# A threshold search by six false-position counts in place of a 31-bit bisection

## The chip, the cores and the metric

One Trainium2 chip, one core. The metric is device time in microseconds (us) of one execution, lower is better.

## What is computed

The kernel takes 2048 tokens of width 1024 through two branches that are added to the input. The part that the change touches is the first branch: for each token it keeps the 1376 of 2752 gate values that are largest in magnitude and sets the others to zero.

```python
s = jax.nn.silu(jnp.einsum('bsh,ih->bsi', x, w_gate))      # 4 x 512 tokens, 2752 units
k = int(K_FACTOR * I)                                      # 1376
_, idx = jax.lax.top_k(-jnp.abs(s), k)
flat = flat.at[rows, idx.reshape(B * S, k)].set(0.0)
s = s * jnp.einsum('bsh,ih->bsi', x, w_up)
return jnp.einsum('bsi,hi->bsh', s, w_down)
...
x = x + _L0_attn_ref(xn, ...) + _L0_ffn_ref(xn, ...)       # second branch: MLP + routed latent + layernorm
```

## The kernel before

**Blocks and granules.** The tokens are worked in four blocks `b` of 512, each as four tiles of 128 tokens. A block is a list of granules `m` (the class `Plan`). A plain granule is one 128-row slice of weights: TensorE makes 4 tiles x 3 matmuls of 512 columns with it, the three being the high-by-high, high-by-low and low-by-high parts of a float32 product (`product`, L1065 to L1067). In blocks 1 to 3 the gate steps and three of the six up steps go in four "fast" pairs: 28 granules each, seven products (`q`, 0 to 6) of four granules, each granule 2 x 3 matmuls. Granules of products 1, 3, 5 and 6 take "mixed" weights: they are loaded as one float32 tile, ScalarE writes its high part (L1026), GpSimd then subtracts to get the low part (L850; in pairs 0 to 2, VectorE makes it for product 6, L1542), and only then can TensorE use the granule. In block 0 every weight is split into its two parts on the chip: while the search runs, GpSimd alone does it, with a `tensor_scalar` (L841) and a `tensor_tensor` (L845) per granule.

**Order.** There is no scheduler. Each engine walks over the same granules and, at the granules that `Plan` names, emits its other work in a fixed order; it then runs in order and waits on semaphores alone. An engine can run ahead of TensorE in this list, or fall behind. ScalarE also evacuates banks: latent (L973), hidden as relu (L982) and square (L994), routed (L986). There are two sets of four PSUM banks, and most steps alternate between them, so a step's banks must be read before the next but one opens.

**The search.** Once all magnitudes `mag` of a block are there (2816 per token, 64 of them padding of -1), the threshold `thr` is found bit by bit from bit 30 down: 31 steps. In each, VectorE counts two token tiles (`search_bit`, L1414) and ScalarE the other two (`count`, L901, a Sign with an accumulated sum); both read `cand`. Then `settle` refuses or keeps the bit with two instructions on 128x4 elements (L1403, L1406). After the last, `drop_ties` counts four tiles once more (L1422) and enters a branch only if more than 1376 are left. `mask` (L1481) applies the threshold, and GpSimd multiplies gate by up (L874) before TensorE turns the product for the last matmuls.

**Where the steps stand.** In block 0 the search begins at granule 52 and its steps are three granules apart. In blocks 1 to 3 it begins ten granules after pair 2 ends, that is at granule 9 of the 28 of the last fast pair (counted from 0); the next steps are 7 and 14 granules later, then every 11/4 granules. The third step would stand in the middle of the last mixed granules, and one line moves ScalarE's part of it to the end of the fast part:

```python
            self.count_at[last] = self.count_at.pop(steps_at[2])
```

## Time and profile before

| | |
|---|---|
| runs | 2320.54 us median of 3 (2317.87 to 2321.05) |
| profiled execution, span from first to last instruction | 2316.5 us |
| its own time with what lies around the span | not given with the profile; the median is 4.0 us above the span |
| TensorE busy | 2300.8 us (99%) |
| VectorE, ScalarE, GpSimd busy | 1674.1, 1112.2, 927.2 us |
| granted TensorE clock | full in all 40 slices |

Engines in the rows are PE (TensorE), DVE (VectorE), ACT (ScalarE), POOL (GpSimd). Matmuls are pipelined: one has a duration of 0.39 us, but the next starts about 0.23 us after it, so durations overlap and the starts are what to read. A row names a source line, the operation, the tiles written and read, shape and number of instructions.

### The profile page before, as it was taken

How to read it: one execution, taken by the hardware profiler on the slowest of the kernel's cores; microseconds unless marked ns; L12 is line 12 of the kernel's file. 1: busy time of each engine (PE TensorE's matmuls, PEld its weight loads, DVE VectorE, ACT ScalarE, POOL GpSimd, SP SyncE). 2: the span in 40 equal slices, each digit the busy share in tenths (PEclk: the TensorE clock that was granted, in tenths of full speed). 3: DMA queues.
4: the chain of work that ended last, by engine and by line, in shares of the span. 5: the costliest groups of instructions: out<-in, count | busy, mean ns of one | idle time of the engine just before them, and what ended most of it. 6: DMA issues, size and time to landing. Idle time of an engine off the chain costs nothing.

```text
span 2316.5 us, 27959 instructions
## 1 busy us (share of the span) xinstructions
PE 2300.8 (99%) x10432; PEld 1912.1 (83%) x10432; DVE 1674.1 (72%) x1834; ACT 1112.2 (48%) x1307; POOL 927.2 (40%) x746
## 2 busy tenths in 40 slices
PE   8999999999999999999999999999999999999999
PEld 6888888888888888888888888888888888888887
DVE  4349999986366999998334599998723569999850
ACT  3247776223243688822124379780213457976110
POOL 5468988797354321333024423035004441302600
PEclk9999999999999999999999999999999999999999
DMA  7798988868899765575678875556567886555655
GB/s 285 276 402 315 334 320 305 266 238 310 300 361 331 244 227 191 195 248 178 235 232 277 283 253 193 197 193 242 203 221 254 282 268 239 192 192 195 232 191 179
DMA packets 202184, 583.61 MB, mean 252 GB/s; under 512 B 21568, under 2 KB 30784, under 8 KB 200512
## 3 DMA queue, kind: packets, MB, share of 16 engines
q1 hardware_dynamic: 202048, 581.82, 72.8%
q8 instruction: 83, 1.36, 0.2%
q14 instruction: 53, 0.43, 0.1%
HBM read 446.40 MB, written 135.33 MB: 251 GB/s over the span
## 4 chain that ended last, share of the span: by engine, by line
PE 82%; DVE 10%; DMA 3%; issue 2%; ACT 1%; SPq 1%; POOL 1%; DVEq 0%; ACTq 0%
PE bank L1065 26%; PE bank L1067 26%; PE bank L1066 26%; DVE junk_v L1414 3%; DVE prod L1481 2%; PE bank L1085 2%; DVE junk_v L1422 2%; DMA mixed_w<-mixes 1%; DMA split_w<-w 1%; DVE prod L1344 1%; PE bank L1076 1%; DVE acc L1385 0%; DMA w<-mixed_w 0%; SPq L631 0%; SPq L627 0%
## 5 line engine op out<-in xcount | busy, mean ns | idle before, releaser
L1414 DVE TENSOR_SCALAR_CACHE_REDUCE junk_v<-mag,cand 128x2816 bf16<-128x2816 f32 x248 | 780.3, 3146 | 8.8
L901 ACT ACTIVATE junk_s<-mag,cand 128x2816 uint8<-128x2816 f32 x248 | 655.9, 2645 | 191.6 <-DVE cand L1406 172.9
L1065 PE MATMUL bank<-w,tok 128*128 128x512 f32 (+1 forms) x808 | 309.9, 384 | 0.2 <-POOL w L845 0.2
L1067 PE MATMUL bank<-w,tok 128*128 128x512 f32 (+1 forms) x808 | 308.3, 381 | 0.0
L1066 PE MATMUL bank<-w,tok 128*128 128x512 f32 (+1 forms) x808 | 308.0, 381 | 0.0
L845 POOL TENSOR_TENSOR w<-raw,w 128x512 fp32r<-128x512 f32 (+1 forms) x196 | 267.9, 1370 | 76.5 <-ACT w L889 66.7
L1065 PE MATMUL bank<-w,prod_t 128*128 128x512 f32 x672 | 269.4, 401 | 0.0
L1067 PE MATMUL bank<-w,prod_t 128*128 128x512 f32 x672 | 262.8, 391 | 0.0
L1066 PE MATMUL bank<-w,prod_t 128*128 128x512 f32 x672 | 261.9, 390 | 0.0
L859 POOL TENSOR_TENSOR squares<-squares 128x512 f32<-128x512 f32 x64 | 67.4, 1054 | 463.9 <-ACT hidden L994 463.9
L1065 PE MATMUL bank<-tok,w 128*128 128x512 f32 x640 | 249.0, 389 | 0.0
L1066 PE MATMUL bank<-tok,w 128*128 128x512 f32 x640 | 249.0, 389 | 0.0
L1067 PE MATMUL bank<-tok,w 128*128 128x512 f32 x640 | 249.0, 389 | 0.0
L1054 ACT ACTIVATE prod_t<-bank 128x512 fp32r<-128x512 f32 x88 | 52.4, 596 | 346.4 <-PE bank L1085 346.4
L850 POOL TENSOR_TENSOR w<-w 128x512 fp32r<-128x512 f32 x96 | 149.1, 1576 | 137.6 <-ACT w L1026 137.3
L1065 PE MATMUL bank<-w,hidden 128*128 128x512 f32 x512 | 199.2, 389 | 0.0
L1066 PE MATMUL bank<-w,hidden 128*128 128x512 f32 x512 | 199.2, 389 | 0.0
L1067 PE MATMUL bank<-w,hidden 128*128 128x512 f32 x512 | 199.2, 389 | 0.0
L874 POOL TENSOR_TENSOR prod<-prod,mag 128x512 f32<-128x512 f32 x88 | 130.9, 1509 | 145.2 <-DVE prod L1481 144.9
L1065 PEld LDWEIGHTS bank<-w,tok 128*128 128x128 f32 x808 | 151.7, 188 | 27.0 <-POOL w L845 0.5
L1067 PEld LDWEIGHTS bank<-w,tok 128*128 128x128 f32 x808 | 151.6, 188 | 26.9
L1066 PEld LDWEIGHTS bank<-w,tok 128*128 128x128 f32 x808 | 151.7, 188 | 26.1
(166 smaller groups left out, 4066.5 us busy)
## 6 DMA issues: line engine op xcount, KB each, us to landing
w<-split_w SPq DMA_DIRECT2D x498, 512.0 KB, 3.4
split_w<-w SPq DMA_DIRECT2D x188, 512.0 KB, 5.3
w_more<-split_w SPq DMA_DIRECT2D x66, 512.0 KB, 5.3
w<-mixed_w SPq DMA_DIRECT2D x126, 256.0 KB, 3.6
w_more<-mixed_w SPq DMA_DIRECT2D x66, 256.0 KB, 3.5
rows<-x_dram SPq DMA_DIRECT2D x32, 512.0 KB, 5.4
raw<-w_down_dram SPq DMA_DIRECT2D x44, 256.0 KB, 4.1
raw<-w_up_dram SPq DMA_DIRECT2D x40, 256.0 KB, 3.2
```

The source lines that it names most:

```text
L845: pool.tensor_tensor(lo, words, hi, ALU.subtract).then_inc(lo_ready, 1)
L850: pool.tensor_tensor(slot_of(g)[:, 1, :], slot_of(g)[:, 1, :].bitcast(F32), slot_of(g)[:, 0, :], ALU.subtract).then_inc(pool_lo, 1)
L859: pool.tensor_tensor(squares[:, n, :], squares[:, n, :], squares[:, n, :], ALU.mult).then_inc(squared, 1)
L874: pool.tensor_tensor(prod[:, c, :, units], prod[:, c, :, units], mag[:, c, :, units], ALU.mult).then_inc(prod_ready, 1)
L901: act.activation(junk_s[:, :, :], mag[:, :, t, :], ACT.Sign, scale=-1.0, bias=cand[:, t:t + 1], accum_out=cnt[:, t:t + 1]).then_inc(counte ...
L1054: act.activation(prod_t[0][:, c, :], banks[bank][:, :], ACT.Copy).then_inc(operand_hi, 1)
L1065: pe.matmul(out, left[0], right[0], start=first, stop=False)
L1066: pe.matmul(out, left[0], right[1], start=False, stop=False)
L1067: return pe.matmul(out, left[1], right[0], start=False, stop=last)
L1085: last = pe.transpose(banks[bank][:, t * P:(t + 1) * P], prod[:, c, t, :], ident[:, :])
L1414: dve.tensor_scalar(junk_v[:, :, :], mag[:, :, t, :], cand[:, t:t + 1], float(1 - (GATED - KEPT)), ALU.is_lt, ALU.add, accum_out=cnt[:, t: ...
L1422: dve.tensor_scalar(junk_v[:, :, :], mag[:, :, t, :], thr[:, t:t + 1], None, ALU.is_ge, ALU.add, accum_out=cnt[:, t:t + 1]).then_inc(searc ...
```

## The change

The search starts from the mean magnitude of each token: VectorE sums one tile (1 instruction), ScalarE three. Then six counts follow at points found by false position (a secant between an upper and a lower point), each with a `settle` of nine instructions on 128x4 to 128x16 elements. A token whose count comes within 3 of the aim keeps its point. Then for each of the four tiles VectorE zeroes what is not below the point (2816 elements) and takes the eight largest of the rest; the threshold is one of these, chosen by how far the count was off. The 31-step bisection stands only in the branch, entered when two values tie at the threshold or when a token's count is still more than 3 off. ScalarE now counts three token tiles and VectorE one, in every step. The steps are four granules apart in block 0; in blocks 1 to 3 they stand at granules 9 (mean), 16 and 23 of the last fast pair and then every three granules. The line that moved ScalarE's part of the third step is gone.

```diff
+COUNTS = 6
+NEAR = 3
+AIM = KEPT - 1 - NEAR
+ROUND = 1.5 * 2 ** 23
...
-            steps_at += [last + 3 + (11 * k + 3) // 4 for k in range(BITS + 1 - len(steps_at))]
+            steps_at += [last + 3 + 3 * k for k in range(COUNTS + 2 - len(steps_at))]
         else:
             first = last + 5 if later else end[("gate", GC - 2)] + LAG + 1
-            steps_at = [first + 3 * k + (0 if later else k // 8) for k in range(BITS + 1)]
-        self.search_at = {m: k for k, m in enumerate(steps_at[:BITS])}
-        self.search_from, self.search_end = first, steps_at[BITS]
-
-        self.count_at = {m: k for m, k in self.search_at.items()}
-        if later and FAST[b] > SPILLED_PAIR:
-            self.count_at[last] = self.count_at.pop(steps_at[2])
+            steps_at = [first + 4 * k for k in range(COUNTS + 2)]
+        self.mean_at = self.search_from = first
+        self.search_at = {m: k for k, m in enumerate(steps_at[1:COUNTS + 1])}
+        self.search_end = steps_at[COUNTS + 1] + 3 * TILES + 1
+        self.pick_at = {steps_at[COUNTS + 1] + 3 * t: t for t in range(TILES)}
+        self.pick_from = steps_at[COUNTS + 1]
+        self.count_at = {first: -1, **self.search_at}
...
-NV = TILES // 2
+NV = 1
 NS = TILES - NV
 VECTOR_TILES, SCALAR_TILES = range(NV), range(NV, TILES)
+WIDTH = GK * P
+OFF = WIDTH // 2 - AIM
+assert NEAR == 3
...
-                if k or n:
-                    act.wait_ge(counted, (b * BITS + k) * NS + n)
-                act.activation(junk_s[:, :, :], mag[:, :, t, :], ACT.Sign, scale=-1.0,
-                               bias=cand[:, t:t + 1], accum_out=cnt[:, t:t + 1]).then_inc(counted, 1)
+                if b or k >= 0 or n:
+                    act.wait_ge(counted, (b * (COUNTS + 1) + k + 1) * NS + n)
+                if k < 0:
+                    act.activation(junk_s[:, :, :], mag[:, :, t, :], ACT.Copy,
+                                   accum_out=cnt[:, t:t + 1]).then_inc(counted, 1)
+                else:
+                    act.activation(junk_s[:, :, :], mag[:, :, t, :], ACT.Sign, scale=-1.0,
+                                   bias=tried[:, 0, t:t + 1], accum_out=cnt[:, t:t + 1]).then_inc(counted, 1)
...
+            def start_search(b):
+
+                at = b * SEARCHES
+                dve.wait_ge(mag_ready, (b + 1) * MAG_STEPS)
+                dve.memset(ends[:, 0, 0, :], 0.0).then_inc(search, 1)
+                dve.memset(ends[:, 0, 1, :], float(GATED - AIM)).then_inc(search, 1)
+                dve.memset(ends[:, 1, 1, :], -float(AIM)).then_inc(search, 1)
+                for i, t in enumerate(VECTOR_TILES):
+                    dve.wait_ge(search, at + 3 + i)
+                    dve.tensor_scalar(junk_v[:, :, :], mag[:, :, t, :], 1.0, None, ALU.mult, ALU.add,
+                                      accum_out=cnt[:, t:t + 1]).then_inc(search, 1)
+
+            def first_guess(b):
+
+                at = b * SEARCHES + 3 + NV
+                dve.wait_ge(counted, (b * (COUNTS + 1) + 1) * NS)
+                dve.wait_ge(search, at)
+                dve.tensor_scalar(ends[:, 1, 0, :], cnt[:, :], float(PAD), 2.0 / GATED, ALU.add,
+                                  ALU.mult).then_inc(search, 1)
+                dve.tensor_scalar(tried[:, 0, :], cnt[:, :], float(PAD), 0.75 / GATED, ALU.add,
+                                  ALU.mult).then_inc(search, 1)
+
+            def away(b, k):
+
+                dve.wait_ge(counted, (b * (COUNTS + 1) + k + 2) * NS)
+                dve.wait_ge(search, b * SEARCHES + searched(k) + NV)
+                dve.scalar_tensor_tensor(out=tried[:, 1, :], in0=cnt[:, :], scalar=-float(2 * OFF), in1=weight[:, :],
+                                         op0=ALU.add, op1=ALU.mult).then_inc(search, 1)
+
             def settle(b, k):
 
                 at = b * SEARCHES + searched(k) + NV
-                bit = 1 << (BITS - 1 - k)
-                after = cand if k + 1 < BITS else thr
-                dve.wait_ge(counted, (b * BITS + k + 1) * NS)
-                dve.wait_ge(search, at)
-                dve.tensor_scalar(refused[:, :], cnt[:, :], float(PAD + 1), float(bit), ALU.is_gt,
-                                  ALU.mult).then_inc(search, 1)
+                away(b, k)
                 dve.wait_ge(search, at + 1)
-                dve.scalar_tensor_tensor(out=after[:, :].bitcast(I32), in0=cand[:, :].bitcast(I32), scalar=bit >> 1,
-                                         in1=refused[:, :], op0=ALU.bitwise_or, op1=ALU.bitwise_xor).then_inc(search, 1)
-
-            def search_bit(b, k):
+                dve.tensor_scalar(outside[:, 0, :], tried[:, 1, :], NEAR + 0.25, None, ALU.is_gt).then_inc(search, 1)
+                dve.tensor_scalar(outside[:, 1, :], tried[:, 1, :], -NEAR - 0.25, None, ALU.is_lt).then_inc(search, 1)
+                dve.wait_ge(search, at + 3)
+                dve.copy_predicated(ends[:, :, :, :], outside[:, :, None, :].to_broadcast([P, 2, 2, TILES]),
+                                    tried[:, None, :, :].to_broadcast([P, 2, 2, TILES])).then_inc(search, 1)
+                dve.wait_ge(search, at + 4)
+                dve.tensor_tensor(apart[:, :, :], ends[:, 1, :, :], ends[:, 0, :, :], ALU.subtract).then_inc(search, 1)
+                dve.wait_ge(search, at + 5)
+                dve.reciprocal(share[:, :], apart[:, 1, :]).then_inc(search, 1)
+                dve.wait_ge(search, at + 6)
+                dve.tensor_tensor(share[:, :], share[:, :], ends[:, 0, 1, :], ALU.mult).then_inc(search, 1)
+                dve.wait_ge(search, at + 7)
+                dve.tensor_tensor(share[:, :], share[:, :], apart[:, 0, :], ALU.mult).then_inc(search, 1)
+                dve.wait_ge(search, at + 8)
+                dve.tensor_tensor(tried[:, 0, :], ends[:, 0, 0, :], share[:, :], ALU.subtract).then_inc(search, 1)
+
+            def search_step(b, k):
 
                 at = b * SEARCHES + searched(k)
                 for i, t in enumerate(VECTOR_TILES):
                     dve.wait_ge(search, at + i)
-                    dve.tensor_scalar(junk_v[:, :, :], mag[:, :, t, :], cand[:, t:t + 1], float(1 - (GATED - KEPT)),
-                                      ALU.is_lt, ALU.add, accum_out=cnt[:, t:t + 1]).then_inc(search, 1)
+                    dve.tensor_scalar(junk_v[:, :, :], mag[:, :, t, :], tried[:, 0, t:t + 1],
+                                      float(2 * OFF - (WIDTH - AIM)), ALU.is_lt, ALU.add,
+                                      accum_out=cnt[:, t:t + 1]).then_inc(search, 1)
+
+            def last_away(b):
+
+                at = b * SEARCHES + PICKED
+                away(b, COUNTS - 1)
+                dve.wait_ge(search, at - 2)
+                dve.tensor_scalar(share[:, :], tried[:, 1, :], 0.25, ROUND, ALU.add, ALU.add).then_inc(search, 1)
+                dve.wait_ge(search, at - 1)
+                dve.tensor_scalar(share[:, :], share[:, :], ROUND, -1.0, ALU.subtract, ALU.mult).then_inc(search, 1)
...
+            def largest_below(b, t):
+
+                at = b * SEARCHES + PICKED + 2 * t
+                dve.wait_ge(search, at)
+                dve.scalar_tensor_tensor(out=below[:, :, :], in0=mag[:, :, t, :], scalar=tried[:, 0, t:t + 1],
+                                         in1=mag[:, :, t, :], op0=ALU.is_lt, op1=ALU.mult).then_inc(search, 1)
+                dve.wait_ge(search, at + 1)
+                dve.max(largest[:, t, :], below[:, :, :].rearrange("p k n -> p (k n)")).then_inc(search, 1)
...
             def drop_ties(b):
...
+                choose(b)
...
                 with dve.If(excess > 0):
...
+                    with dve.Fori(0, BITS):
...
-                    if m == plan.search_from:
-                        dve.wait_ge(mag_ready, (b + 1) * MAG_STEPS)
-                        dve.memset(cand[:, :].bitcast(I32), 1 << (BITS - 1)).then_inc(search, 1)
+                    if m == plan.mean_at:
+                        start_search(b)
                     if m in plan.search_at:
                         if plan.search_at[m]:
                             settle(b, plan.search_at[m] - 1)
-                        search_bit(b, plan.search_at[m])
+                        else:
+                            first_guess(b)
+                        search_step(b, plan.search_at[m])
+                    if m == plan.pick_from:
+                        last_away(b)
+                    if m in plan.pick_at:
+                        largest_below(b, plan.pick_at[m])
                     if m == plan.search_end:
-                        settle(b, BITS - 1)
                         drop_ties(b)
```

ScalarE, block 1, from the last evacuation before the search to the first plain step, before (`junk_s,cnt` are counts, `w`/`w_more` are high parts of mixed granules, `latent` is the first plain step's evacuation):

```order
L940 ACTIVATE prod<-bank 128x4x128 x2
L901 ACTIVATE junk_s,cnt<-mag,cand 128x2816 x2
L1026 ACTIVATE w_more<-w_more 128x512 x4
L901 ACTIVATE junk_s,cnt<-mag,cand 128x2816 x2
L1026 ACTIVATE w<-w 128x512 x2
L1026 ACTIVATE w_more<-w_more 128x512 x4
L1026 ACTIVATE w<-w 128x512 x2
L901 ACTIVATE junk_s,cnt<-mag,cand 128x2816 x8
L973 ACTIVATE latent_58<-bank 128x512 x4
```

and the same place now:

```order
L969 ACTIVATE prod<-bank 128x4x128 x2
L927 ACTIVATE junk_s,cnt<-mag 128x2816 x3
L1055 ACTIVATE w_more<-w_more 128x512 x4
L930 ACTIVATE junk_s,cnt<-mag,tried 128x2816 x3
L1055 ACTIVATE w<-w 128x512 x2
L1055 ACTIVATE w_more<-w_more 128x512 x2
L930 ACTIVATE junk_s,cnt<-mag,tried 128x2816
L1055 ACTIVATE w_more<-w_more 128x512
L930 ACTIVATE junk_s,cnt<-mag,tried 128x2816
L1055 ACTIVATE w_more<-w_more 128x512
L930 ACTIVATE junk_s,cnt<-mag,tried 128x2816
L1055 ACTIVATE w<-w 128x512 x2
```

Three counts stand where two stood, ahead of the first four high parts and ahead of the last eight; and three more counts now lie between the fourth and the seventh of those eight, where none lay.

VectorE, block 0, one settle and the count after it, before (`cand` is the point tried):

```order
L1379 TENSOR_TENSOR latent_59<-bank,latent_58 128x512 x4
L1403 TENSOR_SCALAR refused<-cnt 128x4
L1406 SCALAR_TENSOR_TENSOR cand<-cand,refused 128x4
L1414 TENSOR_SCALAR junk_v,cnt<-mag,cand 128x2816 x2
```

and now (`tried` is the point tried):

```order
L1408 TENSOR_TENSOR latent_59<-bank,latent_58 128x512 x4
L1451 SCALAR_TENSOR_TENSOR tried<-cnt,weight 128x4
L1459 TENSOR_SCALAR outside<-tried 128x4
L1460 TENSOR_SCALAR outside<-tried 128x4
L1462 COPY_PREDICATED ends<-outside,tried 128x16
L1465 TENSOR_TENSOR apart<-ends 128x8
L1467 RECIPROCAL share<-apart 128x4
L1469 TENSOR_TENSOR share<-share,ends 128x4
L1471 TENSOR_TENSOR share<-share,apart 128x4
L1473 TENSOR_TENSOR tried<-ends,share 128x4
L1480 TENSOR_SCALAR junk_v,cnt<-mag,tried 128x2816
```

Two dependent small instructions between a count and the next became nine, and one large one went.

ScalarE, block 0, from the evacuation of hidden step 1 to that of routed step 0, before:

```order
L982 ACTIVATE squares<-bank 128x512 x4
L994 ACTIVATE hidden_55<-squares 128x512
L901 ACTIVATE junk_s,cnt<-mag,cand 128x2816
L994 ACTIVATE hidden_55<-squares 128x512
L901 ACTIVATE junk_s,cnt<-mag,cand 128x2816
L986 ACTIVATE acc<-bank,route 128x512 x4
```

and now:

```order
L1011 ACTIVATE squares<-bank 128x512 x4
L1023 ACTIVATE hidden_55<-squares 128x512
L930 ACTIVATE junk_s,cnt<-mag,tried 128x2816 x2
L1023 ACTIVATE hidden_55<-squares 128x512
L930 ACTIVATE junk_s,cnt<-mag,tried 128x2816
L1015 ACTIVATE acc<-bank,route 128x512 x4
```

The whole sixth count, three instructions, stands ahead of the evacuation of routed step 0.

## Rows read from the trace of the kernel before

**Rows 1.** The page: span, busy time by engine, granted clock in tenths.

```profile
span 2316.5 us, 27959 instructions
...
PE 2300.8 (99%) x10432; PEld 1912.1 (83%) x10432; DVE 1674.1 (72%) x1834; ACT 1112.2 (48%) x1307; POOL 927.2 (40%) x746
...
PEclk9999999999999999999999999999999999999999
```

**Rows 2.** PE's waits: us in total, times, longest.

```profile
PE bank L1076 <- DVE rows L1235: 8.7, 2, 7.8
PE bank L1065 <- POOL w L850: 1.6, 4, 0.6
```

**Rows 3.** Groups on DVE, whole span: busy us, mean ns of one.

```profile
L1414 DVE TENSOR_SCALAR_CACHE_REDUCE junk_v<-mag,cand 128x2816 bf16<-128x2816 f32 x248 | 780.3, 3146 | 8.8
...
L1422 DVE TENSOR_SCALAR_CACHE_REDUCE junk_v<-mag,thr 128x2816 bf16<-128x2816 f32 x16 | 50.3, 3147 | 0.6
...
L1344 DVE SCALAR_TENSOR_TENSOR prod<-positive,prod 128x2048 f32<-128x2048 uint8 x9 | 23.8, 2643 | 0.0
```

**Rows 4.** ACT in order of time, block 1: start us, us.

```profile
765.20 2.65 ACT L901 ACTIVATE junk_s<-mag,cand 128x2816 uint8<-128x2816 f32 x1 [2.08 <-DVE cand L1564]
768.03 2.65 ACT L901 ACTIVATE junk_s<-mag,cand 128x2816 uint8<-128x2816 f32 x1
770.68 2.18 ACT L1026 ACTIVATE w_more<-w_more 128x512 fp32r<-128x512 f32 x4
...
780.70 1.14 ACT L1026 ACTIVATE w<-w 128x512 fp32r<-128x512 f32 x2
```

**Rows 5.** POOL in order of time, block 1, the first low parts.

```profile
771.37 5.05 POOL L850 TENSOR_TENSOR w_more<-w_more 128x512 fp32r<-128x512 f32 x4 [8.38 <-ACT w_more L1026]
```

**Rows 6.** PE in order of time, block 1: fast granule 12, first plain granule.

```profile
773.12 0.39 PE L1065 MATMUL bank<-w_more,sums 128*128 128x512 f32 x1
...
794.88 0.39 PE L1065 MATMUL bank<-tok,w 128*128 128x512 f32 x1
```

**Rows 7.** DVE in order of time, block 1: first settle.

```profile
772.67 1.28 DVE L1403 TENSOR_SCALAR refused<-cnt 128x4 int32<-128x4 f32 x1
773.99 1.21 DVE L1406 SCALAR_TENSOR_TENSOR cand<-cand,refused 128x4 int32<-128x4 int32 x1
```

**Rows 8.** Blocks 2 and 3: first count on ACT, fast granule 12 on PE.

```profile
1329.35 2.65 ACT L901 ACTIVATE junk_s<-mag,cand 128x2816 uint8<-128x2816 f32 x1 [2.17 <-DVE cand L1564]
...
1337.27 0.39 PE L1065 MATMUL bank<-w_more,sums 128*128 128x512 f32 x1
...
1893.06 2.64 ACT L901 ACTIVATE junk_s<-mag,cand 128x2816 uint8<-128x2816 f32 x1 [2.17 <-DVE cand L1564]
...
1900.98 0.39 PE L1065 MATMUL bank<-w_more,sums 128*128 128x512 f32 x1
```

**Rows 9.** Settles on DVE, groups in 167 to 260 us (block 0).

```profile
L1403 DVE TENSOR_SCALAR refused<-cnt 128x4 int32<-128x4 f32 x10 | 6.8, 685 | 0.5
L1406 DVE SCALAR_TENSOR_TENSOR cand<-cand,refused 128x4 int32<-128x4 int32 x10 | 5.2, 521 | 0.3
```

**Rows 10.** The same in 796 to 850 us (block 1, POOL mostly idle).

```profile
L1403 DVE TENSOR_SCALAR refused<-cnt 128x4 int32<-128x4 f32 x8 | 1.3, 167 | 0.6
L1406 DVE SCALAR_TENSOR_TENSOR cand<-cand,refused 128x4 int32<-128x4 int32 x8 | 1.3, 164 | 0.3
```

**Rows 11.** Groups on ACT in 167 to 260 us (block 0).

```profile
L901 ACT ACTIVATE junk_s<-mag,cand 128x2816 uint8<-128x2816 f32 x22 | 58.2, 2643 | 23.7 <-DVE cand L1406 19.8 <-DVE cand L1564 3.2
L994 ACT ACTIVATE hidden<-squares 128x512 fp32r<-128x512 f32 x8 | 5.0, 625 | 0.0
...
L982 ACT ACTIVATE squares<-bank 128x512 f32<-128x512 f32 x8 | 4.2, 592 | 0.0
...
L973 ACT ACTIVATE latent<-bank 128x512 fp32r<-128x512 f32 x4 | 2.0, 592 | 0.0
```

**Rows 12.** Block 0: first count on ACT; PE opens shared step 0 (granule 80).

```profile
167.84 2.64 ACT L901 ACTIVATE junk_s<-mag,cand 128x2816 uint8<-128x2816 f32 x1 [3.23 <-DVE cand L1564]
...
250.85 0.39 PE L1065 MATMUL bank<-w,hidden 128*128 128x512 f32 x1
```

More of the change, by code:

```diff
@@ L400 @@
 MAG_STEPS = (GC - 1) + 4
+SETTLES = 9
 def searched(k):
[L405 to L408 removed]
+    return 3 if k < 0 else 3 + NV + 2 + k * (NV + SETTLES)
+PICKED = searched(COUNTS - 1) + NV + 3
+SEARCHES = PICKED + 2 * TILES + 9
 def program(nc, x, w_gate, w_up, w_down, up_w, down_w, fc1_w, expert_w, fc2_w, gamma, beta, routed_w, y):
@@ L485, in program @@
         ident = sb("ident", [P, P], F32)
-        junk_v = sb("junk_v", [P, GK, P], BF16)
-        junk_s = sb("junk_s", [P, GK, P], U8)
+        below = sb("below", [P, GK, P], F32)
+        junk_at = nc.sbuf_base - GK * P * 4
+        junk_v = over("junk_v", [P, GK, P], BF16, junk_at)
+        junk_s = over("junk_s", [P, GK, P], U8, junk_at + GK * P * 2)
+        after_at = junk_at + GK * P * 3
+        chosen = over("chosen", [P, TILES, 8], F32, after_at)
+        picked = over("picked", [P, TILES, 8], F32, after_at + 128)
+        runner = over("runner", [P, TILES], F32, after_at + 256)
+        cand = over("cand", [P, TILES], F32, after_at + 288)
+        refused = over("refused", [P, TILES], I32, after_at + 320)
+        taken = over("taken", [P, TILES], I32, after_at + 352)
+        neg = over("neg", [P, TILES], F32, after_at + 384)
+        bit_f = over("bit_f", [P, 1], F32, after_at + 416)
+        bit_i = over("bit_i", [P, 1], I32, after_at + 448)
+        ends = sb("ends", [P, 2, 2, TILES], F32)
+        tried = sb("tried", [P, 2, TILES], F32)
+        outside = sb("outside", [P, 2, TILES], I32)
+        apart = sb("apart", [P, 2, TILES], F32)
+        share = sb("share", [P, TILES], F32)
+        weight = sb("weight", [P, TILES], F32)
+        place = sb("place", [P, 8], F32)
+        largest = sb("largest", [P, TILES, 8], F32)
         thr = sb("thr", [P, TILES], F32)
-        cand = sb("cand", [P, TILES], F32)
         cnt = sb("cnt", [P, TILES], F32)
-        refused = sb("refused", [P, TILES], I32)
-        taken = sb("taken", [P, TILES], I32)
         extra = sb("extra", [P, TILES], F32)
@@ new lines, in choose @@
+            def choose(b):
+                at = b * SEARCHES + PICKED + 2 * TILES
+                dve.wait_ge(search, at)
+                dve.tensor_tensor(chosen[:, :, :], place[:, None, :].to_broadcast([P, TILES, 8]),
+                                  share[:, :, None].to_broadcast([P, TILES, 8]), ALU.is_equal).then_inc(search, 1)
+                dve.wait_ge(search, at + 1)
+                dve.tensor_tensor(picked[:, :, :], chosen[:, :, :], largest[:, :, :], ALU.mult).then_inc(search, 1)
+                dve.wait_ge(search, at + 2)
+                dve.tensor_reduce(thr[:, :], picked[:, :, :], AX.X, ALU.add).then_inc(search, 1)
+                dve.wait_ge(search, at + 3)
+                dve.tensor_tensor(picked[:, :, 0:7], chosen[:, :, 0:7], largest[:, :, 1:8], ALU.mult).then_inc(search, 1)
+                dve.wait_ge(search, at + 4)
+                dve.tensor_reduce(runner[:, :], picked[:, :, 0:7], AX.X, ALU.add).then_inc(search, 1)
+                dve.wait_ge(search, at + 5)
+                dve.tensor_tensor(extra[:, :], thr[:, :], runner[:, :], ALU.is_equal).then_inc(search, 1)
+                dve.wait_ge(search, at + 6)
+                dve.tensor_reduce(most[:, 0:1], extra[:, :], AX.X, ALU.max).then_inc(search, 1)
+                dve.wait_ge(search, at + 7)
+                dve.transpose(most_t[:, :], most[:, :]).then_inc(search, 1)
+                dve.wait_ge(search, at + 8)
+                dve.tensor_reduce(ties[:, :], most_t[:, :], AX.X, ALU.max).then_inc(search, 1)
@@ L1519, in _ @@
             dve.memset(most[:, :], 0.0).then_inc(constants_set, 1)
-            dve.wait_ge(constants_set, 1)
+            dve.memset(weight[:, 0:NV], -1.0).then_inc(constants_set, 1)
+            dve.memset(weight[:, NV:TILES], -0.5).then_inc(constants_set, 1)
+            for i in range(8):
+                dve.memset(place[:, i:i + 1], float(i - NEAR if i < 7 else 100)).then_inc(constants_set, 1)
+            dve.wait_ge(constants_set, 11)
             normalise(0, 0, 1)
```

41 lines of the change are left out of this document (24 added, 17 removed).

## The prediction

> **What bounds the kernel now.** I read the page first: TensorE is busy for 2300.8 of 2316.5 us at full clock, so the search is hidden unless an engine that feeds TensorE comes late [rows 1]. Busy time alone hides gaps in overlapped matmuls, so I looked at its waits next: 8.7 us at the start of the program, and 1.6 us for low parts of mixed weights made by GpSimd (L850) [rows 2]. Then at its starts: from fast granule 12 to the first plain granule of block 1 it takes 794.88 - 773.12 = 21.76 us for 16 granules, 1.36 us each, without a hole, hence 2.72 us for a plain granule [rows 6]. The reader is to see that nothing is to be won from less search work except those few microseconds, and that every delay of what TensorE waits for is paid in full, since it never catches up.
>
> How near is such a delay? In block 1 ScalarE starts its two counts at 765.20 us, and only after both, at 770.68, makes the high parts of granules 12 to 15 [rows 4]. GpSimd makes the first low part from 771.37; four take 5.05 us, 1.26 each, so it is done at 772.63 [rows 5]. TensorE opens granule 12 at 773.12 [rows 6]. **0.5 us is all the slack.** Blocks 2 and 3 have the same distance from first count to granule 12: 7.92 us, as block 1 has [rows 4, 6, 8].
>
> **Removed.** VectorE had 248 counts of 3.15 us and 16 last counts [rows 3]; 28 large passes and 32 picking instructions replace them. ScalarE's 248 counts become 84. As TensorE hides all of it, the gain is nothing, at most the 1.6 us of [rows 2]. I take 0.
>
> **Term 1, blocks 1 to 3, three counts in front of mixed granules.** A count costs ScalarE 768.03 - 765.20 = 2.83 us [rows 4]. From the order of the changed kernel:
>
> - Mean: three instead of two, and two more memsets (0.2 us, estimated): 765.4 + 8.5 = 773.9. First high part (a quarter of 2.18 us, plus its fill, 0.6) done at 774.5, first low part at 775.8: granule 12 starts about 2.8 us late. GpSimd's 1.26 us per granule then keeps up with 1.36.
> - Count at granule 16: ScalarE 776.0 to 784.5, high parts of 20 to 23 until 786.7. Granule 20 was due at 773.12 + 8 x 1.36 = 784.0, is now due at 786.8, and its low part comes at 786.5: no more loss. Before, those parts began at 780.70 [rows 4].
> - Settle, from 784.6: nine dependent instructions. Undisturbed they cost 0.165 us and a gap of about 0.04 each, 1.85 us in all [rows 10]. But GpSimd makes four low parts back to back from 785.2 to 790.3. In that same situation the two small instructions of the first settle took 1.28 and 1.21 us, not 0.17, and ended at 773.95 and 775.20, just behind the ends of GpSimd's instructions (771.37 + 1.26 n) [rows 5, 7]. Three of the nine get through before GpSimd starts; of the other six, all but the reciprocal wait for one GpSimd instruction each. `tried` is ready at about 790.4.
> - Count at granule 23, in the middle of the last eight mixed granules, where the removed line had kept it away: ScalarE needs 790.4 to 793.2 for the first tile, then the part of granule 24, low part at 795.1, against a due time of 792.2: 2.9 us more. The second and third tile stand before 25 and 26 and cost 2.83 + 0.6 = 3.4 us of ScalarE per granule of 1.36, 2 us more each. The last two parts follow at once. TensorE leaves the fast part at about 804.6 in place of 794.88: **9.8 us**.
>
> With an undisturbed settle (`tried` at 786.5) the same sum gives 1.2 + 2.0 in place of 2.9 + 2 + 2, in all 6.0 us. These are the ends, 6.0 and 9.8; I take 9.8, because the disturbed rows are from the same place. Three blocks: **29.4 us** (18 to 30).
>
> **Term 2, block 0.** GpSimd splits all weights here and is seldom idle, and the settles show it: 0.685 us for the first of the two small instructions and 0.52 for the second, against 0.167 and 0.164 [rows 9, 10]. Nine of them, eight disturbed: 0.69 + 7 x 0.52 + 0.16 + 9 x 0.035 = 4.8 us. ScalarE's list: mean from 168.0 [rows 12], 8.5 us; guess 1.3; count 8.5; latent evacuation 2.0 and VectorE's part behind it 0.6 [rows 11]; settle 4.8; count 8.5; settle 4.8; count 8.5 (to 215.6); relu of hidden 2.0; count with a square [rows 11] from settle's end at 220.4, 9.1; settle 4.8; count with a square 9.1 (to 243.4); relu of hidden step 1, 2.0; settle beside it; sixth count 248.2 to 257.3 with its square. Only then comes the evacuation of routed step 0 (0.7 for its first bank): 258.0. TensorE opens shared step 0 into that bank at 250.85 [rows 12]. **7.2 us.** (Relu of hidden step 1 frees its first bank at 244.0, for granule 76 due at 250.85 - 4 x 2.72 = 240.0: 4 of the 7 us are lost there already.) Lower end: settles of 1.85 us take 15.7 us off, no wait. Upper end: each of eight small instructions waits for a whole GpSimd instruction (about 1 us, midway between 0.6 and 1.3), settle 8.5 us, five settles, 18 us more: 25.
>
> The SBUF page of the Trainium skill (Who interferes with whom) says that a VectorE instruction with two SBUF inputs, or in a 2-port mode, and a GpSimd instruction that reads SBUF exclude each other for their whole length, while counts with an accumulator do not. By that rule the settles behave as in my upper end when GpSimd never pauses, and [rows 5, 7] agree; [rows 9] show about half of it, since GpSimd pauses in block 0.
>
> **Picks.** Two passes per tile. The nearest row for the first is 2.275 to 2.64 us for 2048 elements [rows 3], so 3.1 to 3.6 for 2816; the eight-largest pass has no row of that size: from 3.1 (one element at a time, as a count) to twice that. 25 to 40 us per block, then nine small instructions. In blocks 1 to 3 they end by about 905 us at the latest (851 for the last count, 40, and settles); the first bank behind them is shared step 0's, wanted again at 804.6 + 48 x 2.72 = 935: hidden. In block 0 they hold up GpSimd for 12 us, whose lead on TensorE I take as a few granules: 0 to 5 us, taken as 0, since the waits of term 2 let GpSimd get ahead first.
>
> **What is behind the waiting VectorE in blocks 1 to 3.** After the fast part a step is 8.5 + 1.85 us against 8.16 for three granules. Behind it stands the latent evacuation, at about 840.5; its banks are wanted at 804.6 + 16 x 2.72 = 848.1. Hidden by 7 us; with settles over 3.5 us this would wait too.
>
> **Sum.** 2316.5 + 29.4 + 7.2 = 2353.1 us of span, and 4.0 us above the span as the median of before stands: **2357, I say 2356 us**. This kernel's runs tell 0.2% (4.6 us) from no change.
>
> **Rivals.**
> 1. *Settles undisturbed in the fast part*, the block 0 wait small: 3 x 6.0 + 0 to 4, giving 2338 to 2343. For it: GpSimd takes only 1.26 us at a time. Against it: [rows 7]. 0.2.
> 2. *Block 0 much worse*: settles at their upper end, picks delaying GpSimd: 2320.5 + 29.4 + 18 to 28 = 2368 to 2378. 0.14.
> 3. *Search hidden, no change or faster* (other side): ScalarE's late start is taken up if the first high parts need not wait, that is if the distance from first count to granule 12 exceeded 8.7 + 0.6 + 1.3 = 10.6 us; it is 7.92 [rows 4, 6]. The search would then be free and the 1.6 us of [rows 2] gone: 2319. Only if the mean pass cost under 1.9 us per tile. 0.04 for no change, 0.01 for faster.
> 4. *The change doesn't do what it says*: six counts do not bring every token within 3, and a block takes the branch, 31 x (4 x 3.15 + 2) = 450 us, some 100 of it hidden: 2700 or more. Worked in float32 on the reference's inputs, 11 of 2048 tokens are more than 3 off after the fifth count, none after the sixth, and no threshold ties. On 16 other draws 3 of 64 blocks would fail. It falls in only if ScalarE's sum of magnitudes is off. 0.05.
>
> Forecast, 2346 to 2366: 0.56. The range of 8 in 10 reaches to rivals 1 and 2: 2335 to 2372. Slower 0.94, same 0.05, faster 0.01, from the same cases.
>
> **What would show it.** In each of blocks 1 to 3 TensorE waits for low parts (L850's place) at fast granules 12, 24, 25 and 26, 2.8, 2.9, 2 and 2 us; one ScalarE count between the parts of 23 and 24; small instructions of 1.2 us in the settle before it. In block 0 a wait of TensorE for the relu and then for routed's evacuation, at 240 to 258 us. ScalarE and VectorE busy time down to some 670 and 1040 us with no gain. Wrong if TensorE shows no wait at granule 12 (term 1), if settles in block 0 take 2 us (term 2), or if VectorE runs thousands of instructions in the branch.

## The result, and the profile after

The changed kernel takes **2357.54 us** (median of 4 runs, 2356.5 to 2363.61) against 2319.2 us for the kernel before on the same chips (4 runs, 2317.78 to 2321.05): ratio **1.0172, 95% interval 1.0157 to 1.0186**, slower. Forecast were 2356 us, 2335 to 2372.

The page of its profiled execution (2358.46 us), lines as in [rows 1]:

```profile
span 2356.7 us, 26924 instructions
...
PE 2314.2 (98%) x10432; PEld 1917.6 (81%) x10432; DVE 1039.0 (44%) x1384; ACT 671.0 (28%) x979; POOL 945.0 (40%) x746
...
PEclk9999999999999999999999999999999999999999
```

VectorE lost 635 us of work and ScalarE 441, and the program is 40.2 us longer. In tenths the granted clock still looks full everywhere. TensorE's longest waits, as in [rows 2] (us in total, times, longest):

```profile
PE bank L1094 <- POOL w_more L875: 14.1, 9, 2.2
PE bank L1105 <- DVE rows L1264: 8.6, 2, 7.7
PE bank L1094 <- POOL w L870: 6.7, 4, 4.0
PE bank L1094 <- POOL w L875: 4.9, 7, 1.5
PE bank L1094 <- ACT acc L1015: 3.6, 1, 3.6
```

The 8.6 us at the start were there before. L875 is the low part of mixed weights (before L850), L870 that of block 0's weights (L845), L1015 the evacuation of routed (L986). New are 14.1 + 4.9 - 1.6 = 17.4 us in the fast parts and 3.6 + 6.7 = 10.3 us in block 0: 27.7 of 40.2. The page of waits does not show the rest.

To find it I set the start of each matmul against that of the same matmul before. This lag grows in two kinds of places only: **15.0 us in block 0** (from 250 to 296 us) and **9.2, 8.4 and 8.3 us in the fast parts** of blocks 1 to 3, 25.9 together; elsewhere it stays within 1 us. TensorE in order of time at the end of block 1's fast part (start us, us):

```profile
809.62 0.50 PE L1094 MATMUL bank<-w_more,tok 128*128 128x512 f32 x1 [2.19 <-POOL w_more L875]
...
812.76 0.80 PE L1094 MATMUL bank<-w_more,tok 128*128 128x512 f32 x1 [1.36 <-POOL w_more L875]
813.36 0.63 PE L1095 MATMUL bank<-w_more,tok 128*128 128x512 f32 x1
813.78 0.63 PE L1096 MATMUL bank<-w_more,tok 128*128 128x512 f32 x1
...
819.64 0.39 PE L1094 MATMUL bank<-tok,w 128*128 128x512 f32 x1
```

The reader is to see two things. TensorE waits for low parts; and behind the last wait matmuls start 0.42 us apart (813.36 to 813.78) instead of 0.23: the lower clock level, 1.2 GHz for 2.4. The windows of the same trace show it (from:to, length, busy us of PE, PEld, DVE, ACT, POOL, granted clock, DMA share, GB/s):

```profile
800.00:811.00 11.00, 8.81 (x39) 6.87 (x37) 10.83 (x12) 7.38 (x9) 6.18 (x5) 1.00 0.73 222
811.00:819.70 8.70, 7.11 (x21) 4.90 (x20) 1.25 (x3) 4.03 (x5) 3.77 (x3) 0.61 0.04 8
```

At 0.61 of the clock, 8.7 us lose some 3.4 us. Waits and slow matmuls together make the lag: in the fast parts 25.9 - 17.4 = 8.5 us are slow matmuls, in block 0 15.0 - 10.3 = 4.7. Not all of that is the clock's price: where the next low part is late anyway, a slow matmul only fills time that would have been a wait.

ScalarE and GpSimd in the same place, as in [rows 4, 5]:

```profile
780.78 2.55 ACT L927 ACTIVATE junk_s<-mag 128x2816 uint8<-128x2816 f32 x1 [2.13 <-DVE ends L1431]
...
788.80 2.17 ACT L1055 ACTIVATE w_more<-w_more 128x512 fp32r<-128x512 f32 x4
790.88 2.63 ACT L930 ACTIVATE junk_s<-mag,tried 128x2816 uint8<-128x2816 f32 x1
...
804.96 2.64 ACT L930 ACTIVATE junk_s<-mag,tried 128x2816 uint8<-128x2816 f32 x1 [3.62 <-DVE tried L1473]
...
807.61 0.61 ACT L1055 ACTIVATE w_more<-w_more 128x512 fp32r<-128x512 f32 x1
808.13 2.63 ACT L930 ACTIVATE junk_s<-mag,tried 128x2816 uint8<-128x2816 f32 x1
...
810.75 0.61 ACT L1055 ACTIVATE w_more<-w_more 128x512 fp32r<-128x512 f32 x1
```

```profile
789.49 5.03 POOL L875 TENSOR_TENSOR w_more<-w_more 128x512 fp32r<-128x512 f32 x4 [10.97 <-ACT w_more L1055]
799.86 2.56 POOL L875 TENSOR_TENSOR w<-w 128x512 fp32r<-128x512 f32 x2 [5.33 <-ACT w L1055]
802.36 2.55 POOL L875 TENSOR_TENSOR w_more<-w_more 128x512 fp32r<-128x512 f32 x2
808.30 1.27 POOL L875 TENSOR_TENSOR w_more<-w_more 128x512 fp32r<-128x512 f32 x1 [3.39 <-ACT w_more L1055]
```

Low parts follow high parts by a fill and 1.27 us; a high part of 0.61 us stands behind each count of 2.8. And the settle between the counts, on VectorE, disturbed and, one step later, not:

```profile
799.98 1.21 DVE L1465 TENSOR_TENSOR apart<-ends 128x8 f32<-128x8 f32 x1
801.22 0.18 DVE L1467 RECIPROCAL share<-apart 128x4 f32<-128x4 f32 x1
801.44 1.00 DVE L1469 TENSOR_TENSOR share<-share,ends 128x4 f32<-128x4 f32 x1
802.47 1.21 DVE L1471 TENSOR_TENSOR share<-share,apart 128x4 f32<-128x4 f32 x1
803.72 1.21 DVE L1473 TENSOR_TENSOR tried<-ends,share 128x4 f32<-128x4 f32 x1
...
821.12 0.17 DVE L1465 TENSOR_TENSOR apart<-ends 128x8 f32<-128x8 f32 x1
```

Block 0 holds what I had not sized. GpSimd (three pieces) and then VectorE in order of time. `raw_more` are tiles on which GpSimd makes four subtractions in a row that serve no granule of this stretch:

```profile
251.30 1.04 POOL L884 TENSOR_TENSOR squares<-squares 128x512 f32<-128x512 f32 x1 [4.25 <-ACT hidden L1023]
...
265.73 3.45 POOL L866 TENSOR_SCALAR w<-raw 128x512 fp32r<-128x512 f32 x1
...
273.62 3.98 POOL L870 TENSOR_TENSOR w<-raw,w 128x512 fp32r<-128x512 f32 x1
277.57 0.61 POOL L866 TENSOR_SCALAR w<-raw 128x512 fp32r<-128x512 f32 x1
278.26 1.29 POOL L870 TENSOR_TENSOR w<-raw,w 128x512 fp32r<-128x512 f32 x1
...
284.18 1.28 POOL L849 TENSOR_TENSOR raw_more<-raw_more 128x512 f32<-128x512 f32 x1
...
288.03 1.26 POOL L854 TENSOR_TENSOR raw_more<-raw_more 128x512 f32<-128x512 f32 x1
```

```profile
264.78 3.92 DVE L1497 SCALAR_TENSOR_TENSOR below<-mag,tried 128x2816 f32<-128x2816 f32 x1
268.74 3.10 DVE L1500 MAX8 largest<-below 128x8 f32<-128x2816 f32 x1
...
272.97 3.50 DVE L1497 SCALAR_TENSOR_TENSOR below<-mag,tried 128x2816 f32<-128x2816 f32 x1
```

Under each first pass of a pick (two SBUF inputs) one GpSimd instruction takes 3.3 to 4.0 us instead of 0.6 to 1.3, and ends 0.5 to 1.1 us behind the pass; below I call this a lock. The four locks take 10.5 us of GpSimd above the usual lengths (2.3, 2.8, 2.7 and 2.7). GpSimd had also stood still behind relus that ScalarE owed it: three waits for `hidden`, 8.5 us, of which 3.8 end at 216 us, 4.2 at 251 us and 0.5 at 257 us. And behind the locks come the four subtractions on `raw_more`, 5.1 us. TensorE's longest wait in the picks stands right behind them:

```profile
291.27 0.50 PE L1094 MATMUL bank<-w,hidden 128*128 128x512 f32 x1 [3.99 <-POOL w L870]
```

### The profile page after: what moved, and what is told of

Same layout as the page of the kernel before. It is cut to its first block, busy times and chain, and to the rows that moved or that the text cites. A ratio compares the mean times of both kernels' runs of the same rounds, so it can differ in the third digit from the quotient of the medians.

```text
span 2356.7 us, 26924 instructions
## 1 busy us (share of the span) xinstructions
PE 2314.2 (98%) x10432; PEld 1917.6 (81%) x10432; DVE 1039.0 (44%) x1384; ACT 671.0 (28%) x979; POOL 945.0 (40%) x746
## 3 DMA queue, kind: packets, MB, share of 16 engines
q8 instruction: 83, 1.36, 0.2%
## 4 chain that ended last, share of the span: by engine, by line
PE 87%; ACT 4%; POOL 3%; DVE 3%; issue 2%; DMA 1%; DVEq 0%; POOLq 0%; SPq 0%; ACTq 0%
PE bank L1094 28%; PE bank L1096 28%; PE bank L1095 28%; ACT junk_s L930 2%; PE bank L1114 2%; POOL w L870 1%; ACT junk_s L927 1%; POOL w L866 1%; PE bank L1105 1%; DVE positive L1356 0%; POOL squares L884 0%; DVE prod L1373 0%; DMA w<-mixed_w 0%; POOL w L875 0%; DMA mixes<-w_up_dram 0%
## 5 line engine op out<-in xcount | busy, mean ns | idle before, releaser
L870 POOL TENSOR_TENSOR w<-raw,w 128x512 fp32r<-128x512 f32 (+1 forms) x196 | 274.3, 1403 | 79.6 <-ACT w L914 69.8
L884 POOL TENSOR_TENSOR squares<-squares 128x512 f32<-128x512 f32 x64 | 84.3, 1317 | 430.7 <-ACT hidden L1023 430.7
L1414 DVE TENSOR_TENSOR acc<-bank,acc 128x512 f32<-128x512 f32 x64 | 43.4, 691 | 404.4 <-PE bank L1096 404.4
L1094 PE MATMUL bank<-w,hidden 128*128 128x512 f32 x512 | 201.0, 393 | 10.3 <-POOL w L870 6.7
L930 ACT ACTIVATE junk_s<-mag,tried 128x2816 uint8<-128x2816 f32 x72 | 190.2, 2641 | 71.4 <-DVE tried L1473 67.1
L875 POOL TENSOR_TENSOR w<-w 128x512 fp32r<-128x512 f32 x96 | 146.3, 1547 | 150.0 <-ACT w L1055 149.7
```

Of the source, the lines that this page charges most:

```text
L870: pool.tensor_tensor(lo, words, hi, ALU.subtract).then_inc(lo_ready, 1)
L875: pool.tensor_tensor(slot_of(g)[:, 1, :], slot_of(g)[:, 1, :].bitcast(F32), slot_of(g)[:, 0, :], ALU.subtract).then_inc(pool_lo, 1)
L884: pool.tensor_tensor(squares[:, n, :], squares[:, n, :], squares[:, n, :], ALU.mult).then_inc(squared, 1)
L930: act.activation(junk_s[:, :, :], mag[:, :, t, :], ACT.Sign, scale=-1.0, bias=tried[:, 0, t:t + 1], accum_out=cnt[:, t:t + 1]).then_inc(co ...
L1094: pe.matmul(out, left[0], right[0], start=first, stop=False)
L1414: dve.tensor_tensor(acc[:, t, cols], banks[bank][:, :], acc[:, t, cols], ALU.add).then_inc(bank_emptied[bank], 1)
```

## Experiments

"Block 0" and "fast parts" are the lag of TensorE over the kernel before gained there, in us, in the profiled run. "Ratio" is that to the kernel before on the same chip; e1 to e4 have one run each, against one of 2320.09 us. The slow matmuls behind one and the same wait differ by some 1.6 us from run to run, and some runs lose 5 us at their start (e2, e8), so the places of a single run are compared, and not its time alone.

| run | time, us | ratio, 95% interval | block 0 | fast parts |
|---|---|---|---|---|
| the change | 2357.54 | 1.0172 (1.0157 to 1.0186) | 15.0 | 25.9 |
| e1 search behind the fast part | 2333.01 | one run | 14.8 | 0.0 |
| e2 removed line restored | 2348.57 | one run | 15.6 | 10.2 |
| e3 two tiles on each engine | 2341.62 | one run | 13.5 | 10.2 |
| e4 first pass with one SBUF input | 2353.00 | one run | 7.4 | 26.9 |
| e5 picks 8 granules apart | 2356.6 | 1.0165 (1.0148 to 1.0182) | 12.2 | 25.8 |
| e6 block 0's steps 6 apart | 2343.52 | 1.0107 (1.009 to 1.0124) | 0.0 | 25.8 |
| e7 e1 + e6 + e5 | 2317.8 | 0.9994 (0.9985 to 1.0004) | 0.0 | 0.0 |
| e8 third step behind the fast part | 2343.77 | 1.0103 (1.0086 to 1.012) | 16.4 | 8.6 |
| e9 picks 14 granules later | 2349.02 | 1.0134 (1.0117 to 1.0151) | 7.2 | 25.5 |
| e10 block 0's steps 5 apart | 2349.95 | 1.0134 (1.0117 to 1.0151) | 6.9 | 25.6 |

**e1.** Is all of the 26 us in where the first steps stand?

```diff
-            steps_at = [first, first + 7, first + 14]
-            steps_at += [last + 3 + 3 * k for k in range(COUNTS + 2 - len(steps_at))]
+            first = last + 3
+            steps_at = [first + 4 * k for k in range(COUNTS + 2)]
```

> Blocks 1 to 3 search only after the fast part: first step three granules behind its end, then every four granules; block 0 as in the changed kernel. Theory (ScalarE's counts stand in front of and between the high parts of mixed granules): the fast parts lose nothing, 25.9 us less than the changed kernel, about 2332 us; block 0 still loses 15. Rival (three counts a step are too much for ScalarE anywhere, the loss only moves to the plain steps): above 2345 us, with waits of TensorE for evacuations by ScalarE.

2333.01 us, and the lag does not change by 0.01 us in any of the three fast parts. Term 1 is a matter of place, not of work; nothing behind the fast part pays for the later search. Block 0 still loses 14.8.

**e2.** The removed line alone, restored as quoted above from the kernel before.

> The changed kernel with the removed line back: ScalarE's part of the step at granule 23 stands at the end of the fast part. Theory: the wait at granule 12 (2.2 us) stays, those at 24 to 27 and the slow matmuls behind them go, 6.2 to 7 us in each of three blocks: 2338 to 2340 us. Rival (the disturbed settle of VectorE is what costs, wherever the counts stand): the loss stays near 9 us a block, above 2350.

2348.57 us, above the expectation. 4.8 us of it were lost in the first 40 us of the program, which the edit cannot reach: 2.1 in longer waits of the first transposes for `rows` (10.7 us in 4, in the change 8.6 in 2), and the granted clock was 0.79 from 28 to 36 us, where the change has 1.00. In the fast parts the lag is 3.9, 3.9 and 2.3 us: the waits at granules 24 to 26 are gone, granule 12 is late by 2.2 us as before, the rest is slow matmuls. So the line is worth 4.4 to 6.0 us per block; without the 4.8 us at the start the run would stand at 2343.8, still 4 us over the expectation, which had forgotten the slow matmuls behind granule 12 (1.7 us in two blocks).

**e8.** The whole third step behind the fast part, settle and VectorE's count too: `steps_at = [first, first + 7]` and the rest after `last`.

> Blocks 1 to 3: the third step (mean, first count, second count) stands behind the fast part on both engines; no settle and no count is left among the last mixed granules. Theory (the loss is in counts in front of high parts): granule 12 still costs 2.2 us and the slow matmuls behind it, the 5 to 6 us behind it go, 3 x 2.5 to 4 us remain with block 0's 15: 2343 to 2348. It also tells whether the 5 us lost at the start of the program in the run with the restored line come again (then 2348 to 2353).

2343.77 us (2340.77 to 2347.04), fast parts 2.4, 3.9 and 2.4. It tells the same as e2, so the settle by itself costs nothing where no ScalarE count is queued in front of high parts. The profiled run, the slowest of its four, again lost some 5 us in its first 40 us. Two of its runs are near 2341 us and two at 2346 and 2347, so e2's odd 4.8 are most likely a variation of the start and not the edit's.

**e3.** `NV = 2`, two token tiles on each of ScalarE and VectorE.

> The changed kernel with two token tiles counted by each engine, positions unchanged. Theory: no wait at granule 12 (two counts fit in its 7.9 us), but the step at granule 23 still stands between the parts: 3.8 + 2 us a block, 5 to 6 in place of 8.6, and no wait for routed's evacuation in block 0 (3.8 less); picks as before: 2343 to 2349 us. Rival (only the place of the counts matters, not how many): above 2353.

2341.62 us. No wait at granule 12 (two sums fit in the 7.92 us of [rows 4, 6, 8]), 3.4 us in each block from 24 to 26, no wait for routed's evacuation in block 0, but 13.5 us lost in the picks all the same: GpSimd waits 4.3 us for `hidden`, and as TensorE waits for nothing ahead of the picks, GpSimd comes to them with less in hand than in the change. The time is 1.4 us under the expectation.

**e4.** In the picks, a first pass that reads one SBUF tile:

```diff
-                dve.scalar_tensor_tensor(out=below[:, :, :], in0=mag[:, :, t, :], scalar=tried[:, 0, t:t + 1],
-                                         in1=mag[:, :, t, :], op0=ALU.is_lt, op1=ALU.mult).then_inc(search, 1)
+                dve.tensor_scalar(below[:, :, :], mag[:, :, t, :], tried[:, 0, t:t + 1], None, ALU.subtract, ALU.add,
+                                  accum_out=sink[:, t:t + 1]).then_inc(search, 1)
```

> The picks' first pass reads one SBUF tensor and writes its sum as well (magnitude minus the point, in place of magnitude where it is below the point), as the counts do; same size, same place. The threshold that it yields is another one than the reference's. Theory (in block 0 the first pass keeps GpSimd off SBUF for its 3.1 us, and GpSimd's weight parts come late): the 11.3 us between 254 and 310 us go, 2347 us. Rival (VectorE comes late for something that TensorE needs): no change, 2357.

2353.00 us: block 0 costs 7.4 instead of 15.0, with GpSimd's instructions at their usual length and no wait for L870. VectorE still has its eight long passes in the same places and TensorE never waits for it, so its lateness is not the cause; the lock on GpSimd is. The expectation put too little on what is left: waits of 3.7 and 0.4 for ScalarE, and 3.3 us of slow matmuls behind them.

**e5.** If the locks eat GpSimd's lead, spreading them should help: `gap = 8` in block 0 instead of 3.

> Only the picks of block 0 move apart: 8 granules between two tiles instead of 3. Theory (each pick's first pass holds GpSimd, and four of them 8 us apart use up GpSimd's lead over TensorE): with 21.8 us between them GpSimd regains its lead, the four waits of TensorE for its low parts at 270 to 295 us (6.7 us) go, and the time falls by about 7 us, to 2350. Rival (what costs is not the lead but a lock each time, wherever it falls): same time as the changed kernel, 2357.

2356.6 us, no difference that the runs can show: a miss of the theory as I had put it. One wait of 4.5 us took the place of four:

```profile
PE bank L1095 <- POOL w L871: 4.5, 1, 4.5
PE bank L1095 <- ACT acc L1016: 3.0, 1, 3.0
```

The third pick now fell upon GpSimd's four instructions for `raw_more`, 8.0 us in which it makes no weights; e9 and e10 come back to this. The question taken up next was where GpSimd had lost its lead.

**e6.** Block 0's steps six granules apart: `steps_at = [first + 6 * k for k in range(COUNTS + 2)]`.

> Only the steps of block 0 move apart: 6 granules between two counts instead of 4. Theory (the sixth count stands ahead of routed's evacuation on ScalarE and makes TensorE wait for that bank): no wait for acc at about 250 us, 3.8 us less, while the picks cost their 8 to 11 us as before: 2349 to 2354. Rival (ScalarE is not late, the settles are): the wait only moves to another evacuation, 2357.

2343.52 us, far better than either theory said: block 0 costs nothing. All four locks are there (GpSimd in order of time):

```profile
280.77 3.46 POOL L866 TENSOR_SCALAR w<-raw 128x512 fp32r<-128x512 f32 x1
...
287.55 3.46 POOL L866 TENSOR_SCALAR w<-raw 128x512 fp32r<-128x512 f32 x1
...
296.29 3.47 POOL L866 TENSOR_SCALAR w<-raw 128x512 fp32r<-128x512 f32 x1
...
303.06 3.46 POOL L866 TENSOR_SCALAR w<-raw 128x512 fp32r<-128x512 f32 x1
```

but ScalarE is on time, GpSimd never waits for `hidden` and TensorE waits for nothing. Four locks in this place cost nothing. Nor does GpSimd's wait for ScalarE by itself (e4 has 7.8 us of it and no wait of TensorE for low parts). But this edit changed two things, ScalarE is on time and the picks stand 25 us later, and e9 takes them apart.

**e9.** Counts four apart as in the change, only the picks 14 granules later, where e6 has them: `steps_at[COUNTS + 1] += 14`.

> Block 0 keeps its counts four granules apart, so ScalarE's relu of hidden (at 250.6 us) and routed's evacuation stay late and GpSimd still stands 8 us waiting for that relu; only the picks begin 14 granules later, at the place where they stood without a loss in the run with counts six apart. Theory (GpSimd lost its lead over TensorE to that wait, and the picks' lockouts then fall on an engine without a lead): after 38 us it has the lead again, block 0 loses 3.8 us and the slow matmuls behind it, 7 in place of 15, and the time is 2349 to 2351, with no wait for GpSimd's low parts (L870). Rival (the picks' four lockouts cost 7 us wherever they stand, and six apart helped only by ScalarE): 2357.

2349.02 us, as expected: block 0 costs 7.2, GpSimd has 8.9 us of waits for `hidden`, and TensorE's only waits from 190 to 345 us are

```profile
PE bank L1095 <- ACT acc L1016: 3.7, 1, 3.7
PE bank L1095 <- ACT squares L1012: 0.4, 1, 0.4
```

The locks are all there again (two of 3.46 and two of 4.0 us), ScalarE is as late as in the change, and they cost nothing. The expectation had its number right, but not its reason, that GpSimd "has the lead again" by then. Call lead the time from the end of a low part to TensorE's first matmul with it (each low part goes with twelve matmuls, so the two can be paired in the trace). Ahead of the first lock:

| | lead ahead of first lock, us | waits of TensorE for low parts, us |
|---|---|---|
| the change | 5.5 | 6.7 |
| e3 | 2.3 | 9.5 |
| e5 | 5.5 | 4.5 |
| e10 | 5.6 | 4.7 |
| e9 | 5.0 | 0 |
| e6 | 8.2 | 0 |

In e9 the lead is not larger than in the change. What differs is the work beside: the four subtractions on `raw_more` are over before the first lock (GpSimd in e9), where in the change they follow the last:

```profile
272.90 1.30 POOL L850 TENSOR_TENSOR raw_more<-raw_more 128x512 f32<-128x512 f32 x1
...
281.96 3.46 POOL L867 TENSOR_SCALAR w<-raw 128x512 fp32r<-128x512 f32 x1
```

In the kernel before, where nothing else disturbs, the lead falls from 8.7 to 4.3 us over them, and behind the squares it otherwise grows by some 0.8 us per granule (a high and a low part take 1.96 of 2.72 us). With the four locks' 10.5 us in front of them even that kernel's lead would be 6 us short there: an estimate, as no run has the picks in that place with ScalarE on time.

**e10.** Steps five apart in block 0.

> Counts of block 0 five granules apart instead of four (13.6 us a step against ScalarE's 8.5 and a settle of 5.8 at most, 14.3). Theory (a step must give ScalarE room for three counts, a settle and the evacuations): still a little too short when evacuations of 2 us are added, but the sixth count comes later than the relu of hidden step 1 and routed's evacuation in the order: wait for acc gone or under 1 us, picks at 265 to 300 us cost 0 to 5: 2343 to 2350. Rival (only six will do): 2355 or more.

2349.95 us: no wait for `acc`, GpSimd waits 3.9 us for `hidden` instead of 8.5, and the picks cost 6.9 where 0 to 5 were expected, the time just inside its range. Of the 4.7 us of waits, 4.2 come in one piece, behind `raw_more`, whose first and last subtraction two of the locks hold:

```profile
270.13 4.14 POOL L849 TENSOR_TENSOR raw_more<-raw_more 128x512 f32<-128x512 f32 x1
...
276.86 3.99 POOL L854 TENSOR_TENSOR raw_more<-raw_more 128x512 f32<-128x512 f32 x1
```

The lead was 5.6 us right before, as in the change before its first lock. So the loss follows how many locks stand in front of `raw_more` or on it (four: 6.7 us of waits; three, farther apart: 4.5; two: 4.7; none: 0) and, in the same place, the lead (e3 against the change).

**e7.** The moves of place of e1, e5 and e6 together, the search's work unchanged.

> Three moves at once, the search itself unchanged: blocks 1 to 3 begin their search behind the fast part, block 0 has its steps 6 granules apart and its picks 8. Theory (all of the loss is in where the steps stand): 2316 to 2322, no difference from the kernel before. Rival (some of the loss is in the work itself, or the moved steps collide with what follows them): 2326 or more, with waits at places that had none.

2317.8 us (10 runs), ratio 0.9994 (0.9985 to 1.0004): no difference from the kernel before. Its page has VectorE at 1033.7 us and ScalarE at 673.0 us, and its waits of TensorE are those of before:

```profile
PE bank L1106 <- DVE rows L1265: 8.6, 2, 7.7
PE bank L1095 <- POOL w L876: 1.5, 3, 0.7
```

The search costs nothing if placed well, and gains nothing, as TensorE is busy throughout.

## Why the prediction was right, and where its terms were off

Both mechanisms of the sum, late high parts in the fast parts and the late evacuation in block 0, are in the trace. That the time came within 2 us (2357.5 for 2356) is luck: three terms were too large and one, put at nothing, was 9.6 us.

- **Term 1, 29.4 us: measured 25.9.** Granule 12: 2.8 forecast, 2.2 measured; the three sums took ScalarE 8.0 us (780.78 to 788.80) where I took 8.5, one being 2.55 us where I took a count's 2.65 [rows 4]. Settle with six slow instructions: four were slow, `tried` at 804.96 against a first count at 780.78, 24.2 us later, where the sum had 790.4 - 765.4 = 25.0. Granules 24 to 26: 2.9, 2 and 2 forecast; by their starts (809.62, 812.76 and 815.92 against 789.44, 790.80 and 792.16, the latter from [rows 6] at 1.36 each) 2.3, 1.8 and 1.8, and another 1.0 behind them in slow matmuls. The low clock between them costs little there, since the low parts set the pace; the view of waits alone (2.19, 1.36, 0.2) would have shown too small a loss. e1, e2 and e8 show the two halves, granule 12 and the count at 23, separately.
- **Rival 1 (settles undisturbed)** is out: 5.6 us in block 1 (799.29 to 804.93) against 1.6 one step later. The Trainium skill (SBUF — State Buffer, Who interferes with whom) says that a VectorE instruction with two SBUF inputs contends with a GpSimd instruction that reads SBUF. These rows agree, for instructions on as few as 128x4 elements: 1.00 to 1.21 us each beside GpSimd, 0.16 to 0.17 without.
- **Term 2, evacuation of routed, 7.2 us: measured 3.6 of wait and 1.8 of slow matmuls behind it** (the lag is 5.4 us from 258 us until the picks' first wait). The wait for the relu that was to come first, at 240 us, did not come. The five settles of block 0 took 4.1, 4.4, 1.7, 5.8 and 6.0 us, 22.0 where I had 24.0; one ran undisturbed. The three sums took 8.2 us (168.04 to 176.19) for 8.5. The sixth count was done at 253.8 instead of 257.3, and e3 and e6 show the term gone with two counts or wider steps. (Worked again, the lower end takes 5 x 2.95 = 14.8 us off, not 15.7; it gives no wait either way.)
- **Picks in block 0, "taken as 0": the step that failed.** They cost 15.0 - 5.4 = 9.6 us, 6.7 of it waits for low parts and 2.9 slow matmuls; without the locks (e4) block 0 loses 7.6 less. I had priced the lock itself about right (12 us of VectorE holding GpSimd, 10.5 measured), and the lead too: "a few granules", it was 5.5 us, two of them. I argued that GpSimd gets ahead first, because TensorE waits. It did not: the kernel before has 6.6 us at the same granule, as GpSimd stood behind the same late ScalarE. My check of who waits for ScalarE stopped at TensorE. But this explains 1 us. What the sum left out is that 12 us of locks exceed such a lead, that between two picks GpSimd regains some 2 us, and that `raw_more` takes another 5.1 us right behind. e6 and e9, with `raw_more` in front of the picks, lose nothing to them.
- **Picks in blocks 1 to 3 and the latent evacuation: hidden**, as said. The evacuation began at 850.67, or 835.1 with block 0's lag of 15.5 taken off (840.5 forecast), and no wait came. The eight-largest pass takes 3.10 us for 2816 elements, the lower bound of what I allowed, the pass before it 3.15.
- **The 4.0 us above the span: too large by 2.2.** They came from the median of before against one profiled span; in every run listed with its own span the time is 1.8 to 1.9 us above it (2358.46 for 2356.7 here).
- **Rivals 3 and 4** did not occur: the branch was not entered (VectorE has 1384 instructions in all). Busy times came out at 671 and 1039 us, forecast 670 and 1040. (The cases add up to 0.95 for slower and 0.04 for the same, where the summary says 0.94 and 0.05.)
- Expectations missed: e2 and e4 (too low, slow matmuls forgotten, and e2's start), e3 (1.4 us too high), e5 and e6. The last two because I thought of each pick's lock by itself and not of what else GpSimd has to do around it.

Open: why some runs lose 4.5 to 5 us at the start of the program, why the clock falls behind some waits only, and what the picks would cost in the change's place with ScalarE on time.

## What to carry to other kernels

Where in-order engines feed a full TensorE, less work on the others is worth nothing, while three long instructions in front of a short one that feeds it are paid in full, less the slack (here 0.5 us); compare the distance to the next due part, not busy shares. When an engine will be held or late, list everyone who waits for it, the producers included, and keep an account for each producer: its lead, less every delay and every piece of other work until it can catch up. Delays that such a lead absorbs singly are paid when they fall together, as the four locks and `raw_more` did. Before dropping cheaper work as useless, try moving it: with edits of place alone the same search costs nothing and leaves VectorE 640 us and ScalarE 439 us idle for something else.

## What the hardware showed that I had not expected

- Behind waits of TensorE the granted clock fell. Block 1's window above has 0.61 behind waits of 2.19 and 1.36 us; in block 0 of the run with picks 14 granules later 12 us behind the 3.7 us wait have 0.72. It is full in the next window. With nothing else late there, block 0 lost 3.1 us more than its waits, which the view of waits doesn't show. How much follows a wait is not fixed: the change's wait of 3.6 us there was followed by 1.8 us, and a wait of 2.0 us at granule 12 was followed by 12 us at 1.00 in the change and at 0.86 in e2.

```profile
250.00:262.00 12.00, 8.30 (x26) 6.31 (x25) 2.18 (x2) 9.34 (x15) 10.32 (x11) 0.72 0.71 239
262.00:284.00 22.00, 22.00 (x98) 18.21 (x97) 8.03 (x9) 0.00 (x0) 21.34 (x20) 1.00 0.83 298
```

- The two-input pass itself takes 3.15 us alone and 3.44 to 4.05 us beside a busy GpSimd in the change, which is held in turn: each side waits for the other.
- Small VectorE instructions with one fp32 tensor input were held beside GpSimd too: in block 0 an `outside` of 128x4 (L1460) took 1.27 us at 188.59 us, 0.16 in the undisturbed settle of block 1.
